# First attention layer of a two-layer cross-attention kernel: softmax sums from ones columns beside the values, and the keys' low half taken by VectorE from PSUM

## The chip, the cores and the metric

The kernel runs on one NeuronCore of a Trainium2 chip. The metric is device time in microseconds (us) of one execution of the whole program; lower is better. The core has TensorE (PE, and PEld for its weight loads), VectorE (DVE), ScalarE (ACT), GpSimd (POOL) and SyncE (SP), which here issues the DMAs. Each engine runs its own instruction list in order and waits on semaphores.

## What is computed

The input x has 8 batches of 256x512, the context has the same shape. The change touches the first layer only: attention with 16 heads of depth 16 over 512 positions, whose outputs are a weighted mean and a weighted standard deviation of the values.

```python
q = einsum('oc,bct->bot', Wq, x) + bq ; k, v likewise from kv
attn = softmax(einsum('bhqd,bhdk->bhqk', q * scale, k))       # 8 batches, 16 heads, 512 x 512
mean = einsum('bhqk,bhkd->bhqd', attn, v)
ex2  = einsum('bhqk,bhkd->bhqd', attn, v * v)
std  = sqrt(relu(ex2 - mean * mean))
out  = masked_instance_norm(x) * std + mean
```

A second layer (self attention, cross attention, MLP, each over 8 batches) follows. It isn't changed.

## The kernel before

Layer 0 works in 32 groups (`GROUPS`): 8 batches of 4 groups, each of `HG` = 4 heads. One window `w` has 8 steps `s`. In step N = 8w + s, TensorE makes the scores of group w for one block of 128 queries and two heads (L321, `scores`), in two halves (high and low parts of fp32 kept as fp32r), and, `LAG` = 13 steps later, the same scores the other way round (L333, `turned`: keys on partitions, step M = N - LAG). VectorE takes the row maxima of the first (L429, `maxima`, one reduction of 128x1024 a step); these go through `spread_maxima` (L435) and the item "turn" into the query operand of the second, so that the exponential (L559, `exponentials`, ScalarE, 128x1024 a step) needs no further subtraction. `weighted` (L345) multiplies the exponentials with `v`, which holds 16 columns of values and 16 of squared values for each head: in every second step four matmuls with 32 output columns each, one per head, in the four column groups of the array.

The PSUM banks: 0 to 3 for scores (two sets), 4 and 5 for `turned` (one set), 6 (`VB`) for `weighted`, 7 (`MB`) for all else. What goes through bank 7 is an ordered list of items (L110, `items_at`): "z" at step 0, "turn" at 1, "k" at 2, "q" at 4, "v" at 6. Each item waits for `s_free`, that is, until the item before it was read out. "k" and "q" project the next group's keys and queries, "v" projects values (two times in four windows).

The softmax sums go another way. GpSimd adds the exponentials of two steps (L657, `pairs`: 4 a window), TensorE sums these over partitions with a matrix of ones (item "z": 8 matmuls), ScalarE copies the result (`take_sums`, L601), and SP writes one row for each head to DRAM.

The next group's keys: ScalarE reads the "k" item into `raw_k` with the bias (`take_k`), VectorE rounds it to `k1` (`high_k`, L406, step 3), GpSimd subtracts (`low`, L647), and VectorE makes `k2` from the rest (`low_k`, L412, step 6). The queries go through `take_q`, `high_q` (L417, step 5) and `both_q` (L423, step 6). At the first step of a window TensorE waits for `k1`, `k2`, `q1` and `q2` of the group.

Once a batch: SP loads the next batch's context, x and mask (L229, `load`, in the window w % 4 == 2); VectorE turns the mask into `far` (L395, `masks`) and sums x and its squares; the sums go SP (`z`) - VectorE (`shares`, L483) - SP (`shares0`, then `rz`, a broadcast back); GpSimd multiplies (`finish_shares`, L666, w % 4 == 3), ScalarE squares the mean (`mean_squared`, step 3), GpSimd subtracts (`finish_variance`, L675); one window later ScalarE takes roots (`roots`, L611, step 3 of w % 4 == 0), which needs another activation table, and GpSimd ends with `finish_x`. SP's `regroup` (L234) moves `v_out` (two buffers) to `mean_in` and `second`; for the first group of a batch it waits until `finish_variance` of the batch before has run:

```python
if G == 0 and b:
    eng.wait_ge(s_fin, FINISH * (b - 1) + 3)
```

Of the kernel before, what the change touches and what calls it, by code (L numbers as in the profile page):

```python
# [7 lines left out]
F32 = mybir.dt.float32  # L8
F32R = mybir.dt.float32r
U8 = mybir.dt.uint8  # L10
ALU = mybir.AluOpType
# [89 lines left out]
def layer0(nc, d, g):  # L101

    GROUPS = NB * NG
    LAG = 13
    RING, SUMS, PROBS = 4, 6, 6
# [4 lines left out]
    def items_at(w, s):  # L110

        if s == 0 and 0 <= w - 3 < GROUPS:
            return [("z", w - 3)]
        if s == 1 and 0 <= w - 1 < GROUPS:
            return [("turn", w - 1)]
        if s in (2, 4) and w + 1 < GROUPS:
            return [("k" if s == 2 else "q", w + 1)]
        if s == 6 and w % 4 == 3 and w + 1 < GROUPS:
            return [("v", (w + 1) // 2)]
        if s == 6 and w % 4 == 1 and w < GROUPS:  # L120
            return [("v", w // 4 * 2 + 1)]
        if s == 6 and w == 0:
            return [("v", 0)]
        return []
# [4 lines left out]
    with ExitStack() as ctx:  # L129
# [9 lines left out]
        ones = sb("ones", [P, QD])  # L139
# [14 lines left out]
        v = sb("v", [P, DC, NH, 2 * HD0])  # L154
        prob = sb("prob", [P, PROBS, 2, D])
        pair = sb("pair", [P, SUMS, 2, D])
        v_out = sb("v_out", [P, 2, D])
        z_out = sb("z_out", [P, D])
# [28 lines left out]
        s_pair = sem("pair")  # L187
# [4 lines left out]
        s_low = sem("low")  # L192
# [6 lines left out]
        s_zd = sem("zd")  # L199
# [4 lines left out]
        s_re = [sem(f"re{k}") for k in range(2)]  # L204
# [16 lines left out]

        def rows_of(n):

            return slice(QD * n, QD * (n + 1))

        with nc.Block() as block:
            @block.sync
            def _(eng):
# [5 lines left out]
                def regroup(n):  # L234

                    b, G = n // NG, n % NG
                    eng.wait_ge(s_vout, n + 1)
                    if G == 0 and b:
                        eng.wait_ge(s_fin, FINISH * (b - 1) + 3)
                    for k in range(HG):  # L240
                        head = HG * (G % 2) + k
                        for j, dst in enumerate((mean_in, second)):
                            src = v_out[QD * k + HD0 * j:QD * k + HD0 * (j + 1), n % 2, :]
                            eng.dma_start(dst[HD0 * head:HD0 * (head + 1), G // 2, :], src).then_inc(s_re[n % 2], DMA)

# [8 lines left out]
                for w in range(GROUPS + 4):  # L254
                    n = w - 3
                    b, G = n // NG, n % NG
                    if 0 <= n < GROUPS:
                        taken(eng, "z", n)
                        for k in range(HG):
                            eng.dma_start(d["sums0"][b % 2, HG * G + k:HG * G + k + 1, :], z_out[QD * k:QD * k + 1, :])\  # L260
                               .then_inc(s_zd, DMA)
                        if G == NG - 1:
                            eng.wait_ge(s_zd, (n + 1) * HG * DMA)
                            eng.dma_start(z[:], d["sums0"][b % 2].rearrange("h (a e) -> (h a) e", a=P // NH))\
                               .then_inc(s_z, DMA)
# [4 lines left out]
                    if 0 <= n < GROUPS and G == NG - 1:  # L270
                        eng.wait_ge(s_rz, b + 1)
                        eng.dma_start(d["shares0"][b % 2].rearrange("h (a e) -> (h a) e", a=P // NH), z[:])\
                           .then_inc(s_rd, DMA)
                        if b:
                            eng.wait_ge(s_fin, FINISH * (b - 1) + 2)
                        eng.wait_ge(s_rd, (b + 1) * DMA)
                        for c in range(SB):
                            eng.dma_start(rz[:, c, :], d["shares0"][b % 2, NH // 2 * c:NH // 2 * (c + 1), None, :]
                                          .broadcast_to([NH // 2, HD0, D])).then_inc(s_rw, DMA)
                    if 0 <= n < GROUPS and G == 0:  # L280
                        regroup(n)
                    if 0 <= n + 1 < GROUPS and (n + 1) % NG:
                        regroup(n + 1)
# [3 lines left out]
            def _(eng):  # L287
                def item(name, n):
# [24 lines left out]
                    else:  # L313
                        eng.wait_ge(s_pair, 4 * n + 4)
                        for u in range(2):
                            for k in range(HG):
                                mm = eng.matmul(ps[rows_of(k), MB, :], ones[:], pair[:, (4 * n + 2 * u + k // 2) % SUMS, k % 2, :],  # L317
                                                start=(u == 0), stop=(u == 1))
                    mm.then_inc(s_item, 1)

                def scores(N, half):  # L321

                    n, j, p = N // 8, N % 8 // 2, N % 2
                    for i in range(2):
# [3 lines left out]
                        mm = eng.matmul(ps[:, SC + 2 * p + i, :], lhsT[r, slot, P * j:P * (j + 1)], rhs[r, n % RING, :],  # L328
# [4 lines left out]
                def turned(M, half):  # L333

                    n, c, p = M // 8, M % 8 // 2, M % 2
# [9 lines left out]
                def weighted(M):  # L345

                    n, c = M // 8, M % 8 // 2
                    b, G = n // NG, n % NG
                    eng.wait_ge(s_exp, M + 2)
                    if c == 0:  # L350
                        eng.wait_ge(s_sq, 2 * b + G // 2 + 1)
                        if n:
                            eng.wait_ge(s_vout, n)
                    for k in range(HG):
# [1239 lines left out]
```

## Time and profile before

| | |
|---|---|
| median of 3 runs | 2137.65 us (2135.59 to 2139.13) |
| the profiled execution | 2135.27 us, span 2133.4 us |
| PE / PEld busy | 1855.3 / 1192.9 us (87% / 56%) |
| DVE / ACT / POOL busy | 1422.0 / 999.7 / 708.5 us (67% / 47% / 33%) |
| mean granted TensorE clock | 0.918 of full speed |
| layer 0 | from the start to about 882 us |

Busy shares are means over four stages with different limits, so the stretch of layer 0 has to be read by itself, by its windows. The time of a window is read from one start of TensorE's `scores` after the wait at step 0 to the next.

### The profile page before, as it was taken

To read this page: it belongs to the slowest core of one execution; us is meant where nothing else is said; L and a number is where in the kernel's file an instruction comes from. 1 tells how busy PE (TensorE), PEld (TensorE's weight loads), DVE (VectorE), ACT (ScalarE), POOL (GpSimd) and SP (SyncE) were. 2 spreads that over 40 slices of the span, in tenths; PEclk is the share of its full clock that TensorE was granted. 3 is DMA by queue.
4 is the path that set the end of the run, shared out by engine and by line. 5 is a ranking of instruction groups with operands and counts; after the bars stand their busy time and mean duration, and the time that the engine had idled before them with its cause. 6 is when DMAs were issued, how large, how long until landed. Compare 5 with 4: busy or idle time off the path is not lost. (4 is left out here: it accounts for less than half of the span.)

```text
span 2133.4 us, 36040 instructions
## 1 busy us (share of the span) xinstructions
PE 1855.3 (87%) x12384; PEld 1192.9 (56%) x12384; DVE 1422.0 (67%) x2731; ACT 999.7 (47%) x2224; POOL 708.5 (33%) x557
## 2 busy tenths in 40 slices
PE   6788878787878787399999996999999969999999
PEld 2323222232222232277777774777777739999998
DVE  4877888879797974177777773777777765232232
ACT  1445555545454545165666653655556545121111
POOL 1545565656565656332222221322222203000000
PEclk8888898988888888699999998999999979999999
DMA  3101010110101000432222222322222204000000
GB/s 109 32 11 44 11 42 23 31 33 21 33 24 40 16 17 21 161 91 61 59 59 59 59 60 73 102 75 69 69 74 74 59 28 146 11 10 10 10 10 20
DMA packets 72907, 104.36 MB, mean 49 GB/s; under 512 B 21220, under 2 KB 37096, under 8 KB 72168
## 3 DMA queue, kind: packets, MB, share of 16 engines
q1 hardware_dynamic: 64616, 86.27, 13.9%
q0 software_dynamic: 8192, 16.79, 3.0%
q8 instruction: 59, 0.97, 0.2%
q14 instruction: 40, 0.33, 0.0%
HBM read 39.56 MB, written 4.72 MB: 21 GB/s over the span
## 5 line engine op out<-in xcount | busy, mean ns | idle before, releaser
L663 POOL TENSOR_TENSOR pair<-prob 128x1024 f32<-128x1024 f32 x128 | 316.5, 2477 | 318.3 <-ACT prob L565 318.3
L432 DVE TENSOR_REDUCE nmax<-ps 128x2 f32<-128x1024 f32 x256 | 310.2, 1217 | 133.7 <-PE ps L328 131.1
L565 ACT ACTIVATE prob<-ps 128x1024 f32<-128x1024 f32 x256 | 262.2, 1024 | 216.8 <-PE ps L340 208.0
L328 PE MATMUL ps<-k,q 32*128 32x512 f32 x1024 | 214.4, 499 | 107.0 <-DVE k L414 91.6
L328 PEld LDWEIGHTS ps<-k,q 32*128 32x128 f32 x1024 | 92.4, 209 | 291.6 <-issue 215.5
L1404 ACT ACTIVATE mlp_h<-ps,b 128x256 f32<-128x256 f32 x128 | 53.7, 472 | 266.8 <-PE ps L1339 266.8
L1443 DVE CAST mlp_h_hi<-mlp_h 128x512 fp32r<-128x512 f32 x64 | 30.2, 471 | 218.8 <-ACT mlp_h L1404 218.8
L340 PE MATMUL ps<-q,k 32*128 32x512 f32 x512 | 143.5, 556 | 34.4 <-ACT prob L565 34.0
L1153 ACT ACTIVATE cross_prob<-cross_t,cross_nmax 128x256 f32<-128x256 f32 x256 | 127.6, 502 | 66.8 <-DVE cross_nmax L1052 65.0
L1153 ACT ACTIVATE self_prob<-self_t,self_nmax 128x256 f32<-128x256 f32 x256 | 127.6, 502 | 55.0 <-DVE self_nmax L1052 53.4
L1339 PE MATMUL ps<-mlp_x_hi,mlp_w_hi 128*128 128x256 f32 x512 | 145.9, 285 | 6.5 <-DVE mlp_w_lo L1428 6.5
L355 PE MATMUL ps<-prob,v 128*32 128x512 f32 x1024 | 149.8, 660 | 1.1 <-ACT prob L565 1.1
L1339 PE MATMUL ps<-mlp_x_lo,mlp_w_hi 128*128 128x256 f32 x512 | 146.0, 285 | 0.0
L1339 PE MATMUL ps<-mlp_x_hi,mlp_w_lo 128*128 128x256 f32 x512 | 146.0, 285 | 0.0
L1238 POOL TENSOR_TENSOR cross_low<-cross_low,cross_high 128x512 fp32r<-128x512 f32 x32 | 41.3, 1292 | 314.4 <-DVE cross_high L1064 286.5
L317 PE MATMUL ps<-pair,ones 128*32 128x512 f32 x512 | 106.6, 980 | 24.6 <-DVE v L451 22.7
L949 PE MATMUL ps<-self_xT,w_self 128*128 128x256 f32 x512 | 125.3, 389 | 2.9 <-ACT self_xT L1175 1.1
L1052 DVE CUSTOM_DVE_ANT_0 self_t<-self_t,self_off 128x256 f32<-128x256 f32 x256 | 112.4, 476 | 18.4 <-DVE self_t L1046 0.6
L1238 POOL TENSOR_TENSOR self_low<-self_low,self_high 128x512 fp32r<-128x512 f32 x32 | 40.6, 1268 | 253.1 <-DVE self_high L1064 225.2
L1052 DVE CUSTOM_DVE_ANT_0 cross_t<-cross_t,cross_off 128x256 f32<-128x256 f32 x256 | 109.2, 463 | 18.4 <-DVE cross_t L1046 0.2
L340 PE MATMUL ps<-q2m,k 32*128 32x512 f32 x512 | 113.1, 436 | 0.0
L949 PEld LDWEIGHTS ps<-self_xT,w_self 128*128 128x128 f32 x512 | 93.7, 192 | 20.2 <-ACT self_low L1167 5.1
(182 smaller groups left out, 4367.5 us busy)
## 6 DMA issues: line engine op xcount, KB each, us to landing
self_k_stack<-self_high SPq DMA_DIRECT2D x128, 64.0 KB, 2.1
cross_k_stack<-cross_high SPq DMA_DIRECT2D x128, 64.0 KB, 2.1
mlp_w_in<-in_w SPq DMA_DIRECT2D x32, 256.0 KB, 3.0
c_in<-in_ctx SPq DMA_DIRECT2D x8, 512.0 KB, 3.7
X<-in_x SPq DMA_DIRECT2D x8, 512.0 KB, 4.5
mean_in<-v_out SPq DMA_DIRECT2D x128, 32.0 KB, 2.0
second<-v_out SPq DMA_DIRECT2D x128, 32.0 KB, 2.0
rz<-shares SPq DMA_DIRECT2D x16, 256.0 KB
```

The lines of the kernel that those rows point to most:

```text
L317: mm = eng.matmul(ps[rows_of(k), MB, :], ones[:], pair[:, (4 * n + 2 * u + k // 2) % SUMS, k % 2, :], start=(u == 0), stop=(u == 1))
L328: mm = eng.matmul(ps[:, SC + 2 * p + i, :], lhsT[r, slot, P * j:P * (j + 1)], rhs[r, n % RING, :], start=(half == 0), stop=(half == 1))
L340: mm = eng.matmul(ps[:, ST + i, :], lhsT[r, n % RING, P * c:P * (c + 1)], rhs[r, slot, :], start=(half == 0), stop=(half == 1))
L355: mm = eng.matmul(ps[rows_of(k), VB, :], v[:, c, HG * G + k, :], prob[:, (M + k // 2) % PROBS, k % 2, :], start=(c == 0), stop=(c == DC - 1))
L432: eng.tensor_reduce(nmax[:, n % 2, j, 2 * p:2 * p + 2], ps[:, SC + 2 * p:SC + 2 * p + 2, :], AX, ALU.max, negate=True).then_inc(s_max, 1)
L565: eng.activation(prob[:, M % PROBS, :, :], ps[:, ST:ST + 2, :], ACT.Exp).then_inc(s_exp, 1)
L663: eng.tensor_tensor(pair[:, at % SUMS, :, :], prob[:, M % PROBS, :, :], prob[:, (M + 2) % PROBS, :, :], ALU.add).then_inc(s_pair, 1)
L949: mm = eng.matmul(bank[:, S * T:S * (T + 1)], wt[:, c, P * (2 * n + T):P * (2 * n + T + 1)], src[:, c, :], start=(c == 0), stop=(c == DC - 1))
L1052: ins = eng.tensor_tensor_reduce(t[:, i, k, :], t[:, i, k, :], off[:, j, :], 1.0, NEVER, ALU.add, ALU.min, nmax[:, m % 4, k:k + 1])
L1153: ins = eng.activation(prob[:, m % 2, i, :], t[:, p, i, :], ACT.Exp, scale=-1.0, bias=nmax[:, m % 4, i:i + 1], accum_out=z[:, T % 2, j, 2 ...
L1238: eng.tensor_tensor(low[:, k, :, :], low[:, k, :, :].bitcast(F32), high[:, k, :, :].bitcast(F32), ALU.subtract).then_inc(s_lo.sem, 1)
L1339: mm = eng.matmul(ps[:, HB + n % 2, S * i:S * (i + 1)], w[:, c, col], x[:, c, :], start=(k == 0), stop=(k == len(terms) - 1))
```

## The change

- `v` gets 64 columns for each head: values, squares, and 32 columns of ones that are set once. `weighted` has 64 output columns a matmul, so that a bank of 128 partitions holds two heads; a group of four heads is done in two passes of four steps each. The sums come out of the same matmuls. `pairs`, the item "z", `take_sums`, `pair` and `z_out` are gone.
- Steps are ordered so that the four blocks of one pair of heads follow each other; `LAG` is 12. `v_out` has three buffers (`OUTS`), read out twice a window (steps 1 and 5); `regroup` issues 6 DMAs a pass, sums among them.
- The keys' high and low parts are both made by VectorE straight from PSUM (`high_k`, now two instructions, step 2), `low_k` moves to step 3, `high_q` to 4, `both_q` to 5. `take_k` and GpSimd's `low` are gone.
- Items: "k" at step 1, "turn" at 2, "q" at 3, "v" at 5.
- SP's order: in w % 4 == 1 the whole chain from the sums to `rz` comes before the next window's `load`, where before `load` stood between `z` and its wait for `shares`.

```diff
-    LAG = 13
-    RING, SUMS, PROBS = 4, 6, 6
+    LAG = 12
+    RING, PROBS, OUTS = 4, 6, 3
...
-        if s == 0 and 0 <= w - 3 < GROUPS:
-            return [("z", w - 3)]
-        if s == 1 and 0 <= w - 1 < GROUPS:
+        if s in (1, 3) and w + 1 < GROUPS:
+            return [("k" if s == 1 else "q", w + 1)]
+        if s == 2 and 0 <= w - 1 < GROUPS:
             return [("turn", w - 1)]
...
-        v = sb("v", [P, DC, NH, 2 * HD0])
+        v = sb("v", [P, DC, NH, 4 * HD0])
...
                 def regroup(n):
 
-                    b, G = n // NG, n % NG
+                    b, G, p = n // (2 * NG), n // 2 % NG, n % 2
                     eng.wait_ge(s_vout, n + 1)
-                    if G == 0 and b:
+                    if G == 0 and p == 0 and b:
                         eng.wait_ge(s_fin, FINISH * (b - 1) + 3)
...
+                for w in range(GROUPS + 3):
                     if w % NG == 2 and w + 2 < GROUPS:
                         made(eng, "k", w + 1)
                         eng.wait_ge(s_mask, w // NG + 1)
                         load(w // NG + 1)
...
+                    if 0 <= w - 2 < GROUPS:
+                        n = w - 2
+                        b, G = n // NG, n % NG
+                        regroup(2 * n)
+                        regroup(2 * n + 1)
+                        if G == NG - 1:
+                            for k in range(OUTS):
+                                eng.wait_ge(s_re[k], regrouped(2 * n + 1, k))
+                            eng.dma_start(z[:], d["sums0"][b % 2].rearrange("h (a e) -> (h a) e", a=P // NH))\
+                               .then_inc(s_z, DMA)
+                            eng.wait_ge(s_rz, b + 1)
...
                 def weighted(M):
 
-                    n, c = M // 8, M % 8 // 2
+                    n, c, p = M // 8, M % 4, M % 8 // 4
                     b, G = n // NG, n % NG
-                    eng.wait_ge(s_exp, M + 2)
                     if c == 0:
                         eng.wait_ge(s_sq, 2 * b + G // 2 + 1)
-                        if n:
-                            eng.wait_ge(s_vout, n)
-                    for k in range(HG):
-                        mm = eng.matmul(ps[rows_of(k), VB, :], v[:, c, HG * G + k, :], prob[:, (M + k // 2) % PROBS, k % 2, :],
-                                        start=(c == 0), stop=(c == DC - 1))
+                        if 2 * n + p:
+                            eng.wait_ge(s_vout, 2 * n + p)
+                    for m in range(M, M + 2):
+                        eng.wait_ge(s_exp, m + 1)
+                        for k in range(2):
+                            mm = eng.matmul(ps[2 * QD * k:2 * QD * (k + 1), VB, :], v[:, m % 4, HG * G + 2 * p + k, :],
+                                            prob[:, m % PROBS, k, :], start=(m % 4 == 0), stop=(m % 4 == 3))
                     mm.then_inc(s_pv, 1)
...
                 def high_k(n):
-                    taken(eng, "k", n)
+                    made(eng, "k", n)
                     if n >= RING:
                         eng.wait_ge(s_st, 8 * (n - RING) + 8)
-                    eng.tensor_copy(k1[:, n % RING, :], raw_k[:]).then_inc(s_k1, 1)
+                    eng.tensor_scalar(k1[:, n % RING, :], ps[:, MB, :], b0[:, 1, n % NG:n % NG + 1], None, ALU.add)\
+                       .then_inc(s_k1, 1)
+                    eng.wait_ge(s_k1, n + 1)
+                    eng.scalar_tensor_tensor(out=raw_k[:], in0=ps[:, MB, :], scalar=b0[:, 1, n % NG:n % NG + 1],
+                                             in1=k1[:, n % RING, :].bitcast(F32), op0=ALU.add, op1=ALU.subtract)\
+                       .then_inc(s_free, 1)
...
                 def take_values(n):
-                    eng.wait_ge(s_pv, 4 * n + 4)
-                    if n >= 2:
-                        eng.wait_ge(s_re[n % 2], (n // 2) * 2 * HG * DMA)
-                    eng.activation(v_out[:, n % 2, :], ps[:, VB, :], ACT.Copy).then_inc(s_vout, 1)
+                    eng.wait_ge(s_pv, 2 * n + 2)
+                    if n >= OUTS:
+                        eng.wait_ge(s_re[n % OUTS], n // OUTS * 6 * DMA)
+                    eng.activation(v_out[:, n % OUTS, :], ps[:, VB, :], ACT.Copy).then_inc(s_vout, 1)
```

## Rows read from the trace of the kernel before

**Rows 1.** Stretches of layer 0: bounds, length, busy time by engine, PEclk, DMA share, GB/s.
```profile
100.05:204.18 104.13, 81.79 (x533) 29.95 (x534) 80.11 (x77) 48.66 (x57) 56.01 (x26) 0.84 0.09 25
204.18:716.27 512.09, 407.37 (x2660) 150.29 (x2661) 432.13 (x441) 261.93 (x305) 299.92 (x135) 0.85 0.10 28
716.27:793.04 76.77, 61.63 (x391) 21.98 (x392) 63.14 (x68) 39.47 (x46) 41.08 (x19) 0.83 0.07 18
793.04:844.66 51.62, 40.03 (x254) 12.91 (x254) 28.05 (x40) 30.03 (x33) 35.07 (x15) 0.84 0.09 21
```

**Rows 2.** Groups of instructions by line: busy, mean ns; idle before, with releasers.
```profile
L663 POOL TENSOR_TENSOR pair<-prob 128x1024 f32<-128x1024 f32 x128 | 316.5, 2477 | 318.3 <-ACT prob L565 318.3
L328 PE MATMUL ps<-k,q 32*128 32x512 f32 x1024 | 214.4, 499 | 107.0 <-DVE k L414 91.6 <-DVE nmax L432 15.4
L451 DVE TENSOR_TENSOR v<-ps,bv 128x512 f32<-128x512 f32 x16 | 10.9, 683 | 0.0
```

**Rows 3.** Timeline at a window's end (start, length, engine): DVE beside GpSimd.
```profile
406.15 2.82 DVE L414 SCALAR_TENSOR_TENSOR k<-raw_k,row,far 128x512 fp32r<-128x512 f32 x1
...
409.07 0.80 PE L328 MATMUL ps<-k,q 32*128 32x512 f32 x2 [4.01 <-DVE k L414]
```

**Rows 4.** Timeline of one window, w = 14: its first steps.
```profile
357.34 0.74 DVE L414 SCALAR_TENSOR_TENSOR k<-raw_k,row,far 128x512 fp32r<-128x512 f32 x1
...
366.53 0.50 PE L309 MATMUL ps<-q,ident_r 128*128 128x512 f32 x1
...
367.36 0.50 PE L328 MATMUL ps<-k,q 32*128 32x512 f32 x2
...
370.03 0.50 PE L328 MATMUL ps<-k,q 32*128 32x512 f32 x2
```

**Rows 5.** The same window, a step with `weighted` and the next with "q".
```profile
370.70 1.06 PE L355 MATMUL ps<-prob,v 128*32 128x512 f32 x8
370.81 1.22 DVE L432 TENSOR_REDUCE nmax<-ps 128x2 f32<-128x1024 f32 x1 [1.45 <-PE ps L328]
370.85 1.02 ACT L565 ACTIVATE prob<-ps 128x1024 f32<-128x1024 f32 x1
...
371.92 0.50 PE L340 MATMUL ps<-q,k 32*128 32x512 f32 x2
...
372.58 1.98 PE L300 MATMUL ps<-X,w 128*128 128x512 f32 x4
```

**Rows 6.** Timeline of the drain, where "z" met the full clock.
```profile
811.39 1.92 PE L317 MATMUL ps<-pair,ones 128*32 128x512 f32 x16
...
813.25 0.50 PE L340 MATMUL ps<-q,k 32*128 32x512 f32 x2
```

**Rows 7.** SP's queue and what stands beside it, windows w = 14 and 15.
```profile
370.13 0.41 SPq L230 DMA_DIRECT2D c_in<-in_ctx  x1
...
378.91 0.34 SPq L272 DMA_DIRECT2D shares<-z  x1
...
380.42 1.29 SPq L278 DMA_DIRECT2D rz<-shares  x2
...
405.75 0.58 SPq L244 DMA_DIRECT2D mean_in<-v_out  x1
```

**Rows 8.** DMA issues: count, KB each, median us from issue to landing.
```profile
m_in<-in_mask SPq DMA_DIRECT2D x8, 64.0 KB, 4.4
...
mean_in<-v_out SPq DMA_DIRECT2D x128, 32.0 KB, 2.0
```

**Rows 9.** Timeline at layer 0's end: from the sums to their shares' use.
```profile
857.70 1.31 SPq L278 DMA_DIRECT2D rz<-shares  x2
862.93 2.34 POOL L671 TENSOR_TENSOR mean_a<-mean_in,rz 128x1024 f32<-128x1024 f32 x1 [15.38 <-DMA rz<-shares]
```

**Rows 10.** Timeline of w = 16, step 3: the roots in ScalarE's queue.
```profile
421.38 1.28 ACT L614 ACT_TABLE_LOAD   x1
...
425.14 1.02 ACT L565 ACTIVATE prob<-ps 128x1024 f32<-128x1024 f32 x1
```

More of the change, by code:

```diff
@@ L153, in layer0 @@
         wide = sb("wide", [P, DC, P], F32R)
-        v = sb("v", [P, DC, NH, 2 * HD0])
+        v = sb("v", [P, DC, NH, 4 * HD0])
         prob = sb("prob", [P, PROBS, 2, D])
-        pair = sb("pair", [P, SUMS, 2, D])
-        v_out = sb("v_out", [P, 2, D])
-        z_out = sb("z_out", [P, D])
+        v_out = sb("v_out", [P, OUTS, D])
         z = sb("z", [P, NH * D // P])
@@ L186, in layer0 @@
         s_exp = sem("exp")
-        s_pair = sem("pair")
         s_pv = sem("pv")
@@ L203, in layer0 @@
         s_rw = sem("rw")
-        s_re = [sem(f"re{k}") for k in range(2)]
+        s_re = [sem(f"re{k}") for k in range(OUTS)]
         s_mask = sem("mask")
@@ L220, in made, with regrouped @@
             eng.wait_ge(s_item, number[(name, n)] + 1)
+        def regrouped(n, k):
+            return (n - k + OUTS) // OUTS * 6 * DMA
         def rows_of(n):
@@ L269, in _ @@
                         load(w // NG + 1)
[L270 to L283, printed above, removed]
+                    if 0 <= w - 2 < GROUPS:
[9 more added lines that the diff above has]
+                            eng.wait_ge(s_rz, b + 1)
+                            eng.dma_start(d["shares0"][b % 2].rearrange("h (a e) -> (h a) e", a=P // NH), z[:])\
+                               .then_inc(s_rd, DMA)
+                            if b:
+                                eng.wait_ge(s_fin, FINISH * (b - 1) + 2)
+                            eng.wait_ge(s_rd, (b + 1) * DMA)
+                            for c in range(SB):
+                                eng.dma_start(rz[:, c, :], d["shares0"][b % 2, NH // 2 * c:NH // 2 * (c + 1), None, :]
+                                              .broadcast_to([NH // 2, HD0, D])).then_inc(s_rw, DMA)
                 eng.wait_ge(s_big, 4 * DMA)
@@ L312, in item @@
                                             stop=(j == DC - 1))
[L313 to L318, printed above, removed]
                     mm.then_inc(s_item, 1)
                 def scores(N, half):
-                    n, j, p = N // 8, N % 8 // 2, N % 2
+                    n, j, p = N // 8, N % 4, N % 8 // 4
                     for i in range(2):
@@ L617, in _ @@
                 eng.wait_ge(s_b0, 1)
-                take_k(0)
                 take_q(0)
@@ L655, in squares @@
                     eng.tensor_tensor(v[:, :, half, HD0:2 * HD0], vv, vv, ALU.mult).then_inc(s_sq, 1)
-                def pairs(n, u, p):
-                    at, M = 4 * n + 2 * u + p, 8 * n + 4 * u + p
-                    eng.wait_ge(s_exp, M + 3)
-                    if at >= SUMS:
-                        made(eng, "z", (at - SUMS) // 4)
-                    eng.tensor_tensor(pair[:, at % SUMS, :, :], prob[:, M % PROBS, :, :], prob[:, (M + 2) % PROBS, :, :],
-                                      ALU.add).then_inc(s_pair, 1)
                 def finish_shares(b, k):
                     if k == 0:
-                        for n in range(2):
-                            eng.wait_ge(s_re[n], (b + 1) * NG // 2 * 2 * HG * DMA)
+                        for k in range(OUTS):
+                            eng.wait_ge(s_re[k], regrouped(2 * NG * b + 2 * NG - 1, k))
                         eng.wait_ge(s_rw, (b + 1) * SB * DMA)
```

114 lines of the change are left out of this document (37 added, 77 removed).

## The prediction

> **What bounds the kernel now.** Only layer 0 changes, so I read it by itself, first by stretches. Between TensorE's first `scores` of w = 8 and of w = 28 lie five batches in 512.09 us, 102.4 each or 25.6 a window [rows 1]. VectorE is busy 432 of these 512 us, TensorE 407, at a mean granted clock of 0.85: part of the time runs at the lower level (1.2 instead of 2.4 GHz). Neither engine is full, so the order of work decides. The groups by line say where TensorE stands: 91.6 us idle in front of `scores`, waiting for the next group's `k2` [rows 2]. The timeline of a window's end shows why: `low_k` comes last before the window starts, takes 2.82 us beside a GpSimd addition [rows 3], and 0.74 us where none runs [rows 4]. After 4.01 us of waiting TensorE's matmuls take 0.80 us instead of 0.50 [rows 3, 4]: it has also lost its clock. So a window is eight steps plus a stall of about 4 us and its echo.
>
> **The steps, priced at full clock.** The four pieces of `scores` and `turned` fill 0.67 us before `weighted` begins (370.03 to 370.70) [rows 4, 5]. The exponential starts at 370.85, takes 1.02, and the next `turned` starts at 371.92, 1.89 after the step's own start at 370.03: no step can be shorter, since banks 4 and 5 exist once and `turned` and the exponential take turns in them [rows 4, 5]. A step with "k" or "q" is 0.67 + 1.95 = 2.62 (one such step: 2.67 [rows 4]). "turn" adds 0.83 (366.53 to 367.36) [rows 4].
>
> **What is removed.** GpSimd's `pairs` (128 of 2477 ns [rows 2]) were never the last to arrive; they count by what they did to `low_k` and the other VectorE operations beside them. The item "z" (8 matmuls with four column groups at work) takes 1.86 at full clock (811.39 to 813.25) [rows 6] and goes. The wait for `k2` goes: `low_k` now follows at step 3, `both_q` at step 5, two steps ahead of need. In all, the stall and its clock echo of every window.
>
> **What is added.** (1) `weighted`: four matmuls with 32 columns take one turn of the array's four column groups, about 1.0; now two matmuls share it, so four of them make two turns. I price them as what "z" shows, two turns in 1.86, less a little, 1.84 [rows 6]: 0.85 more than before, 128 times. The bounds: 1.0 if width were free [rows 5], and 3.9 if each matmul of 64 columns ran alone like those of "k" (two in 1.95 [rows 4, 5]). I take 1.84, since time per turn doesn't depend on the columns used in any of these rows. With `scores` the step is 2.51.
> (2) VectorE's `high_k` reads bank 7 twice, after `maxima` of step 2. A PSUM operand of that size costs 0.68 [rows 2]; two cost 1.36. "turn" is next in bank 7, in the same step 2. Its wait ends at 0.78 (scores done, 370.81 less 370.03) + 1.22 + 1.36 + 0.04 = 3.4 after the step's start [rows 4, 5], where TensorE is free at 2.51: a new stall of 0.9 in every window, and the step is 3.4 + 0.83 = 4.23.
> (3) ScalarE loses `take_k` and `take_sums`, gains a second `take_values`: nothing, it stays off the path in plain windows.
>
> The Trainium skill (SBUF — State Buffer, Who interferes with whom) says that a VectorE operation with two SBUF inputs, or in a two-port mode, waits for a GpSimd one in full; the trace agrees, 2.82 against 0.74 [rows 3, 4]. By it the new subtraction, with one input in PSUM, would never wait.
>
> **A plain window:** steps 0, 4, 6: 3 x 2.51; steps 1, 3: 2 x 2.62; step 2: 4.23; steps 5, 7: 2 x 1.89. Sum 20.8, against 25.6. Two "v" items a batch add 0.75 each: 4 x 20.8 + 1.5 = 84.7 a batch, 17.7 less than now. VectorE's work fits: no step asks more than 3.4 of it.
>
> **Once a batch, four places give much of it back.**
> (a) The load. Before, SP issued it at 370.13, ahead of `shares` at 378.91 and `rz` at 380.42 [rows 7]. Now it comes behind them. Counted from step 5 of w % 4 == 2: `maxima` ends at 2.0, `both_q` and `shares` at 3.2, `rz` is issued at 3.2 + 1.5 = 4.7, `load` at 6.0, its last part at 7.0, landing 4.4 later = 11.4 [rows 7, 8]; but `rz` itself lands 5.2 after its issue [rows 9], about 9.9, and the load's bytes queue behind it. I take 12.5. TensorE wants it at step 1 of the next window, at 1.89 + 2.51 + 1.89 + 2.51 + 0.67 = 9.5. Stall 3.0, in six batches, plus 0.6 for VectorE's `masks`, which wait for the same load and stand in front of `maxima` of step 2.
> (b) `take_values` at step 5 of w % 4 == 3. With three buffers it needs the one whose `regroup` is the first of the batch, and that waits for `finish_variance`. From the start of step 4: `take_q` and then `mean_squared` end at 1.85 (about 0.7 and 1.05 in ScalarE's queue; the exponential of step 4, due at 0.82, is 1.0 late, and 0.6 of that is slack of a 2.51 step over 1.89: 0.4 lost), `finish_variance` at 4.4 (2.34 when nothing is beside it [rows 9], 2.5 taken), then six DMAs of up to 0.6 each [rows 7], the last landing 2.0 after its issue [rows 8]: 8.9. ScalarE is there at 4.8 and has the exponential of step 6 queued behind; TensorE stands at `weighted` of step 6 from 6.2 until 9.6. Stall 3.4 + 0.4, in seven batches. Before, this regroup began at 405.75 [rows 7], with a whole window left.
> (c) `roots` at step 3: table, roots, table, then the exponential 3.76 later (421.38 to 425.14) [rows 10]. It now comes behind `take_q`, so the exponential due at 0.82 starts at 0.8 + 3.76 = 4.56, 3.7 late; less 0.6 of slack TensorE loses 3.1 (it loses some of that before too, inside the 102.4).
> (d) Each of these three pauses is as long as the one after which the matmuls slowed [rows 3]. I take 1.7 for each dip of the clock, an estimate between nothing and the 2.5 that a whole step of `weighted` would lose at half clock: 5.1.
> A batch: 84.7 + 3.6 + 3.8 + 3.1 + 5.1 = 100.3, against 102.4: 2.1 less.
>
> **The sum.** Batches 2 to 6: 5 x 2.1 = 10.5. Batch 1 has no roots: 84.7 + 7.4 + 3.4 = 95.5 against 104.1: 8.6 [rows 1]. Windows 28 to 30 (no load): 62.4 + 0.8 + 3.1 + 1.7 = 68.0 against 76.8: 8.8 [rows 1]. From w = 31 to the last exponential: 51.6 now [rows 1]; about 55.4 by the same steps, for "k", "q" and their stall were already absent and `weighted` costs more: minus 3.8. Behind it the last pair additions and "z" drop out of the chain of sums, and a regroup comes in: 1.8 less. The first batch (pipeline filling, hardly a stall or a "z") at nothing. 10.5 + 8.6 + 8.8 - 3.8 + 1.8 = 26. The profiled execution took 2135.27 (span 2133.4), 2.4 below the median of 2137.65, within their spread. 2135.3 - 26 = 2109; I say 2109.
>
> **The rivals.**
> 1. The giving back doesn't happen: the load's bytes overtake, or the regroup of (b) is early enough, and the clock stays high. Then a batch is 84.7 + 3.1 = 87.8: 14.6 less, five times 73, batch 1 19.4, windows 28 to 30 10.9, the end nothing: 103 less, 2032. For it: medians of DMA latency come from busy times. Against it: both orders are fixed in the code, and the sums are several us over.
> 2. Slower, by the price of 64 columns. If two 64-column matmuls don't share the array fully, each `weighted` costs more than 1.84; at 1.84 + 26/128 = 2.04 the gain is gone, at 3.9 the kernel takes 2109 + 128 x 2.06 = 2373, at a halfway 2.9 it is 2245. Nothing in the trace shows a 64-column tile. Against it: the two ends in the trace both fill the array.
> A page weighs for it: the Trainium skill (TensorE: Matmul & The Clock Gate, Measured speedup vs the span model) gives 2.38 times for three tiles of 32 columns, not 3. Here four tiles gain more, 4 in 1.0 against 2 in 1.95 at full width, 3.9 times, so the trace doesn't bear it out. By that shortfall (0.79) `weighted` would take about 2.3, and the kernel, by the rows, 2109 + 128 x 0.46 = 2168.
> 3. Slower, by the batch stalls: if load and regroup each cost 3 us more than I say (a load that shares the queue with `rz` throughout, the wait for it also holding VectorE), thirteen times 3 are 39: 2148. It decides from 2 us more on.
> 4. It doesn't do what it says: the stall in front of a window stays at 4 us because another of the four semaphores comes last. In the 29 windows from w = 2 on that prepare a next one, 29 x 4 = 116 more than my sum: 2225. Against it: `both_q` is done at step 5.
>
> **How the numbers follow.** The forecast, a gain mostly given back, 0.5 (its own range 2085 to 2132); rival 1, whole or in good part, 0.2; rival 2 0.12 (its page's version 0.04 of that); rival 3 0.13; rival 4 0.05. About 0.2% (4 us) is what a measurement of this kernel can tell from no change. Faster: 0.2 + nine tenths of 0.5 + a bit = 0.66; within: 0.12; slower: 0.22. The range takes in rival 1 and rival 3: 2030 to 2152.
>
> **What would show it.** Right: `weighted` steps of 2.5; a 0.9 us wait in front of "turn" on VectorE's `high_k`; no wait of `scores` for `k2`; one wait a batch of "k" for the load and one of `weighted` for `v_out`; `low_k` at 0.74; GpSimd busy less than half of now; a mean clock of 0.85 to 0.95 in layer 0. Wrong: `weighted` steps of 3 or more; a layer 0 that ends before 830 us or after 890 (now about 882).

## The result, and the profile after

The changed kernel takes 2145.99 us (median of 18 runs, 2137.45 to 2155.15); the kernel before takes 2137.77 in the same rounds (18 runs, 2135.59 to 2140.21). The ratio is 1.0038, with a 95% interval of 1.0026 to 1.0050: slower by 0.4%, where 2109 and a gain of 1.3% were forecast.

The page of the changed kernel, its first part (engine, busy us, share, instructions) and the costliest groups of layer 0 (busy, mean ns | idle before, releaser):

```profile
span 2135.6 us, 34721 instructions
PE 1868.5 (87%) x11872; PEld 1214.7 (57%) x11872; DVE 1288.7 (60%) x2763; ACT 973.5 (46%) x2192; POOL 343.5 (16%) x397
...
L345 PE MATMUL ps<-prob,v 128*64 128x512 f32 x1024 | 270.7, 652 | 24.8 <-issue 20.8
L317 PE MATMUL ps<-k,q 32*128 32x512 f32 x1024 | 201.3, 469 | 8.7 <-DVE nmax L427 4.6
```

By shares, the change did what it says. GpSimd's busy time halves (708.5 to 343.5), VectorE loses 133 us, and the idle time in front of `scores` falls from 107.0 us [rows 2] to 8.7. Not even the clock speaks against it: over the program the granted clock rises from 0.918 to 0.948. Yet nothing is won, so the question is where the 98 us of removed stall went, and with it the forecast gain of 26. The groups of layer 0 by line, of the same trace, name the heirs:

```profile
L295 PE MATMUL ps<-c_in,w 128*128 128x512 f32 x128 | 77.6, 738 | 36.4 <-DMA m_in<-in_mask 36.4
L588 ACT ACTIVATE v_out<-ps 128x512 f32<-128x512 f32 x64 | 37.9, 593 | 31.3 <-DMA second<-v_out 30.1 <-PE ps L345 1.2
L304 PE MATMUL ps<-q,ident_r 128*128 128x512 f32 x32 | 16.3, 510 | 29.6 <-DVE raw_k L403 29.6
```

The "k" item waits for the load (11.1 of the 36.4 us at the very start, 25.3 in six batches), the read-out into `v_out` waits for a `regroup` (30.1 in seven batches), and "turn" waits for VectorE's second read of bank 7 (29.6 us over 32 windows, 0.9 in most of them). All three stand in the forecast. So the miss is one of sizes, and it takes an account stretch by stretch.

**The account.** I cut both traces as the forecast did, at TensorE's first `scores` of a window; layer 0 ends where VectorE starts on the next layer's first tile. "Usual" is a second execution of the changed kernel (2144.24 us, e9 below); the first profiled one is the fastest of the 18 and shows only 2.2 of the 8 us.

| stretch | forecast | fastest execution | usual execution |
|---|---|---|---|
| start to w = 4 | 0 | +8.5 | +8.5 |
| w = 4 to 8 (batch 1) | -8.6 | -5.9 | -4.2 |
| w = 8 to 28 (batches 2 to 6) | -10.5 | -1.2 | +3.4 |
| w = 28 to 31 | -8.8 | -7.2 | -8.4 |
| w = 31 to the end of layer 0 | +2.0 | +4.1 | +6.3 |
| the rest of the program | 0 | +4.0 | +3.3 |
| sum | -26 | +2.2 | +9.0 |

(The spans are 2133.4 before, 2135.6 and 2142.4 after; the rows are rounded. The bounds before are 100.05, 204.18, 716.27, 793.04 [rows 1] and 882.7; in the changed kernel they are 108.50, 206.72, 717.60, 787.13 and 880.9, in e9 108.50, 208.47, 723.99, 792.41 and 888.4.)

**A plain window is as forecast.** Timeline of the changed kernel from step 0 of w = 17 to the "q" item at step 3 (start, length, engine, line, output and inputs, idle before):

```profile
439.73 1.94 PE L345 MATMUL ps<-prob,v 128*64 128x512 f32 x8
...
441.59 0.50 PE L317 MATMUL ps<-k,q 32*128 32x512 f32 x2
...
444.17 0.50 PE L317 MATMUL ps<-k,q 32*128 32x512 f32 x2
...
446.09 0.74 DVE L400 TENSOR_SCALAR k<-ps,b 128x512 fp32r<-128x512 f32 x1
...
446.87 0.75 DVE L403 SCALAR_TENSOR_TENSOR raw_k<-ps,b,k 128x512 f32<-128x512 f32 x1
447.67 0.50 PE L304 MATMUL ps<-q,ident_r 128*128 128x512 f32 x1 [0.89 <-DVE raw_k L403]
...
449.26 1.99 PE L295 MATMUL ps<-X,w 128*128 128x512 f32 x4
...
450.41 0.74 DVE L409 SCALAR_TENSOR_TENSOR k<-raw_k,row,far 128x512 fp32r<-128x512 f32 x1
```

`weighted` occupies 439.73 to 441.59, 1.86 (forecast 1.84). The wait in front of "turn" is 0.89 (0.9). `low_k` takes 0.74, where it took 2.82 beside GpSimd [rows 3]. From one "q" item to the next, windows without a batch's event take 20.95, or 21.72 with "v" (20.8 and 21.5).

### The profile page after: what moved, and what is told of

Same layout as the page of the kernel before. It is cut to its first block and busy times, and to the rows that moved or that the text cites. A ratio compares the mean times of both kernels' runs of the same rounds, so it can differ in the third digit from the quotient of the medians.

```text
span 2135.6 us, 34721 instructions
## 1 busy us (share of the span) xinstructions
PE 1868.5 (87%) x11872; PEld 1214.7 (57%) x11872; DVE 1288.7 (60%) x2763; ACT 973.5 (46%) x2192; POOL 343.5 (16%) x397
## 5 line engine op out<-in xcount | busy, mean ns | idle before, releaser
L345 PE MATMUL ps<-prob,v 128*64 128x512 f32 x1024 | 270.7, 652 | 24.8 <-issue 20.8
L317 PE MATMUL ps<-k,q 32*128 32x512 f32 x1024 | 201.3, 469 | 8.7 <-DVE nmax L427 4.6
L329 PE MATMUL ps<-q,k 32*128 32x512 f32 x512 | 134.4, 521 | 65.7 <-ACT prob L561 65.7
L317 PEld LDWEIGHTS ps<-k,q 32*128 32x128 f32 x1024 | 86.9, 197 | 157.5 <-DVE nmax L427 99.2
L1397 DVE CAST mlp_h_hi<-mlp_h 128x512 fp32r<-128x512 f32 x64 | 30.1, 470 | 218.8 <-ACT mlp_h L1358 218.8
L345 PEld LDWEIGHTS ps<-prob,v 128*64 128x64 f32 x1024 | 66.2, 143 | 154.2 <-issue 147.7
L295 PE MATMUL ps<-c_in,w 128*128 128x512 f32 x128 | 77.6, 738 | 36.4 <-DMA m_in<-in_mask 36.4
L329 PEld LDWEIGHTS ps<-q,k 32*128 32x128 f32 x512 | 49.9, 192 | 98.9 <-ACT prob L561 92.6
L329 PE MATMUL ps<-q2m,k 32*128 32x512 f32 x512 | 105.3, 408 | 0.0
L1293 PEld LDWEIGHTS ps<-mlp_x_hi,mlp_w_hi 128*128 128x128 f32 x512 | 99.0, 193 | 9.5 <-DVE mlp_w_lo L1382 7.4
```

The source lines that it names most:

```text
L295: mm = eng.matmul(bank, (wq if name == "q" else wk)[:, c, P * G:P * (G + 1)], src, start=(c == 0), stop=(c == SB - 1))
L317: mm = eng.matmul(ps[:, SC + 2 * (N % 2) + i, :], lhsT[r, slot, P * j:P * (j + 1)], rhs[r, n % RING, :], start=(half == 0), stop=(half == 1))
L329: mm = eng.matmul(ps[:, ST + i, :], lhsT[r, n % RING, P * c:P * (c + 1)], rhs[r, slot, :], start=(half == 0), stop=(half == 1))
L345: mm = eng.matmul(ps[2 * QD * k:2 * QD * (k + 1), VB, :], v[:, m % 4, HG * G + 2 * p + k, :], prob[:, m % PROBS, k, :], start=(m % 4 == 0) ...
L1293: mm = eng.matmul(ps[:, HB + n % 2, S * i:S * (i + 1)], w[:, c, col], x[:, c, :], start=(k == 0), stop=(k == len(terms) - 1))
```

## The experiments

Single windows are cut here at the starts of the "q" items: window w runs from the "q" of w - 1 to its own. The stall of the load then falls into w % 4 == 3, that of `v_out` (from step 5 of that window) into w % 4 == 0, and that of the roots into w % 4 == 1.

**e1: the load no longer behind `rz`.** The load is issued first, the shares' way out and back (`shares0`, `rz`) moves behind it, out of w % 4 == 1:

```diff
+                def shared_out(b):
+                    eng.wait_ge(s_rz, b + 1)
+                    eng.dma_start(d["shares0"][b % 2].rearrange("h (a e) -> (h a) e", a=P // NH), z[:])\
+                       .then_inc(s_rd, DMA)
...
+                    if w % NG == 2 and 0 <= w - 3 < GROUPS:
+                        shared_out((w - 3) // NG)
```

> The changed kernel with one order on SP put back: the next batch's load is issued before SP waits for the shares, as in the kernel before. Theory 1 (in plain windows the change gains 4 to 5 us each, and it gives that back at three places a batch, each with its echo in the clock): the wait of the k item for the load (25 us over six batches in the trace of after, 3.8 to 4.7 each) is gone, and with the clock echo six windows of 26.0 to 28.1 us between two q items become about 21.3; 6 x 5.5 = 33 us less than the changed kernel's median of 2146, so about 2113. Rival (another wait takes its place: TensorE's doubled weighted sum is the real limit): within 10 us of 2146. The spread of the runs, 18 us in the changed kernel, should shrink if it comes from DMA latencies on the path.

Measured: 2138.07 us (10 runs, 2135.3 to 2150.19), ratio to before 1.0007 [0.9992, 1.0023], 8 us less than the changed kernel and not 33. The rival's number (within 10 us of 2146) came true, but the next limit is not `weighted`, as it had it. The spread did not shrink much either: 15 us over 10 runs. The wait of "k" is gone (11.1 us are left, at the start), and another took its place. Timeline of e1 around step 1 and 2 of w = 19:

```profile
483.74 2.36 POOL L640 TENSOR_TENSOR mean_a<-mean_in,rz 128x1024 f32<-128x1024 f32 x1 [23.80 <-DMA rz<-shares]
...
484.51 1.87 DVE L392 CAST mask<-m_in 128x512 f32<-128x512 uint8 x1
...
486.06 2.53 POOL L642 TENSOR_TENSOR second<-second,rz 128x1024 f32<-128x1024 f32 x1
...
486.42 2.45 DVE L396 TENSOR_SCALAR far<-mask,row 128x512 f32<-128x512 f32 x1
...
488.90 1.22 DVE L431 TENSOR_REDUCE nmax<-ps 128x2 f32<-128x1024 f32 x1
...
491.63 0.80 PE L308 MATMUL ps<-q,ident_r 128*128 128x512 f32 x1 [3.85 <-DVE raw_k L407]
```

`masks` now run at step 1, where GpSimd multiplies in `finish_shares`. They take 1.87 and 2.45 us, `maxima` of step 2 stands behind them, `high_k` behind that, and "turn" waits 3.85 instead of 0.89. The load's stall had been hiding this one: `masks` waited for the same load and then met only the second of GpSimd's two multiplications (the conversion took 1.98 there, `far` 0.55). The wait for `raw_k` sums to 47.5 us here, 18 more than in the changed kernel.

**e2: a fourth `v_out` buffer.** One character, `OUTS = 3` to `OUTS = 4`, so the read-out of a batch's third last pass no longer needs the buffer whose `regroup` waits for `finish_variance`.

```diff
-    RING, PROBS, OUTS = 4, 6, 3
+    RING, PROBS, OUTS = 4, 6, 4
```

> The changed kernel with four v_out buffers instead of three, nothing else. Theory 1: ScalarE's take_values no longer waits for the regroup behind finish_variance (30 us over seven batches, 4.3 each in the trace of after), and the seven windows of 27.1 us become about 21.7: 7 x 5.4 = 38 us less, about 2108. Rival (SP is behind anyway, so the wait comes one buffer later): less than 10 us gained.

Measured: 2109.2 us (4 runs, 2108.18 to 2112.96), ratio 0.9869 [0.9852, 0.9885], 37 less than the changed kernel. The groups of layer 0 in e2 show the one wait gone and the other unchanged or longer:

```profile
L295 PE MATMUL ps<-c_in,w 128*128 128x512 f32 x128 | 78.7, 746 | 40.0 <-DMA m_in<-in_mask 40.0
...
L588 ACT ACTIVATE v_out<-ps 128x512 f32<-128x512 f32 x64 | 37.9, 592 | 1.2 <-PE ps L345 1.2
```

The windows w % 4 == 0 fall from 27.1 to 21.96, so this stall and its clock echo cost 5.2 each, seven times: 36. The forecast had 3.8 + 1.7 = 5.5, and the expectation of 38 us less was met.

**e3: both.**

> Both edits in one: load issued first and four v_out buffers. Theory 1: the gains add, since they lie in different windows: about 71 us less than the changed kernel, about 2075, with 29 windows near 21 us but those with the roots (26.7). Rival: the gains overlap (each dip of the clock is shared by two stalls) and the sum is under 50, over 2096.

Measured: 2091.88 us (4 runs, 2085.96 to 2095.25), ratio 0.9774 [0.9755, 0.9792], between the two expectations. In e3 "turn" waits 3.99 at the same place as in e1: `masks` beside `finish_shares` hold on to 28 us (what e6 wins over e3) of the 45 that lie between e2 and e6.

**e6: `masks` one step earlier.** On top of e3, `masks` move from step 1 to step 7 of the window before, where GpSimd is idle (with the load in time, the mask is there).

```diff
+                        if w % NG == 2 and s == 7 and b + 1 < NB:
+                            masks(b + 1)
...
-                            if s == 1 and b + 1 < NB:
-                                masks(b + 1)
```

> e3_both with the mask work of the next batch (two VectorE instructions) moved from step 1 of the window w % 4 == 3 to step 7 of the window before. In e1 and e3 the wait for the load is gone, but the six windows w % 4 == 3 still take 24.4 to 25.4 us instead of 21: the mask copy (1.9 to 2.0 us there, 0.43 alone) and the far operation (2.45, alone 0.55) meet finish_shares on GpSimd and hold maxima and high_k of step 2, and turn waits 3.9 us. Theory 1, extended (the late load hid this port conflict): these windows fall to about 21.1, and with them the next window's 23.0 by 1 to 2 (its clock dip): 6 x 4 to 6 = 24 to 36 us less than e3's 2092, so 2056 to 2068. Rival (the stall moves on to another VectorE operation of these windows, since GpSimd's five large operations must run somewhere): less than 10 us gained.

Measured: 2063.96 us (4 runs, 2063.67 to 2064.31), ratio 0.9650 [0.9634, 0.9667]. The windows w % 4 == 3 are plain now (20.95). Groups of layer 0 in e6, and behind them the conversion in the changed kernel:

```profile
L308 PE MATMUL ps<-q,ident_r 128*128 128x512 f32 x32 | 16.3, 510 | 29.2 <-DVE raw_k L407 29.2
...
L396 DVE TENSOR_SCALAR far<-mask,row 128x512 f32<-128x512 f32 x8 | 4.4, 546 | 0.3
L392 DVE CAST mask<-m_in 128x512 f32<-128x512 uint8 x8 | 3.4, 422 | 1.4 <-DMA m_in<-in_mask 1.4
```

```profile
L388 DVE CAST mask<-m_in 128x512 f32<-128x512 uint8 x8 | 14.3, 1786 | 18.5 <-DMA m_in<-in_mask 18.5
```

The conversion of the mask takes 422 ns on average, against 1786 in the changed kernel, and 1.87 us in e1's timeline: same instruction, same tile, only the neighbour on GpSimd is gone. The Trainium skill (SBUF — State Buffer, Who interferes with whom) counts conversions and operations with a scalar among those that can take the pair of ports which VectorE shares with GpSimd; the engine that asks second then waits until the other's instruction is over. The traces agree, with 1786 against 422 ns for the one and 2.45 against 0.55 us for the other; in e1 the conversion ends at 486.38 and `far` at 488.87, each 0.3 us behind the end of a GpSimd multiplication (486.10 and 488.59). It is the same rule that I had quoted for `low_k`, not applied to `masks`.

**e7: no square roots in layer 0.** e6 with the two roots of a batch turned into copies, so that the activation table stays. This kernel leaves the square roots of layer 0 out; all other work is there.

```diff
-                    eng.activation(std_a[:], std_a[:], ACT.Sqrt)
-                    eng.activation(x_var[:, b, :], x_var[:, b, :], ACT.Sqrt).then_inc(s_root, 1)
+                    eng.activation(std_a[:], std_a[:], ACT.Copy)
+                    eng.activation(x_var[:, b, :], x_var[:, b, :], ACT.Copy).then_inc(s_root, 1)
```

> e6_mask_early with the two square roots of layer 0 left out (the activations copy instead), which takes away the two changes of the activation table at step 3 of w % 4 == 0 and nothing else; its output is not the reference's. It prices the third place. Theory 1: the six windows with roots (25.7 us in e3) fall to about 21.1 by the two table loads on the path and the clock's echo; 6 x 4.5 = 27 us less than e6. Rival (take_q, mean and root work itself hold ScalarE, not the tables): under 10 us less.

Measured: 2029.42 us (4 runs, 2027.33 to 2033.8), ratio 0.9492 [0.9476, 0.9508]: 34.5 less than e6, 4.9 for each of seven batches. I had expected 27 on record; the forecast's own terms (c) and (d), 3.1 + 1.7 = 4.8, for seven batches, were the better guess. Stretches of e6 and then e7 (length, busy time of PE, PEld, DVE, ACT and POOL, PEclk, DMA share, GB/s):

```profile
200.00:700.00 500.00, 434.40 (x2556) 171.92 (x2552) 359.21 (x507) 270.20 (x314) 73.86 (x37) 0.96 0.11 30
```

```profile
200.00:700.00 500.00, 444.83 (x2722) 178.18 (x2720) 392.52 (x533) 271.33 (x322) 79.88 (x40) 1.00 0.12 32
```

With the last pause gone the granted clock is 1.00 throughout: every dip that e6 still had in the steady part of this layer came with the roots.

**e8: items reordered.** e6 with "turn" at step 1, "k" at 3, "q" at 5 and "v" at 7, and VectorE's steps moved along, so that `high_k` is not between "k" and "turn" within two steps.

```diff
-        if s in (1, 3) and w + 1 < GROUPS:
-            return [("k" if s == 1 else "q", w + 1)]
-        if s == 2 and 0 <= w - 1 < GROUPS:
+        if s in (3, 5) and w + 1 < GROUPS:
+            return [("k" if s == 3 else "q", w + 1)]
+        if s == 1 and 0 <= w - 1 < GROUPS:
...
-                            if s == 2:
+                            if s == 4:
                                 high_k(w + 1)
```

> e6_mask_early with the items in another order: turn at step 1, k at 3, q at 5, v at 7 (before 2, 1, 3, 5), with the VectorE and ScalarE work that belongs to them moved along (values one step later, high_q and both_q together at step 6). It takes turn out of the same step as high_k's two reads of bank 7. Theory 1: step 1 hides the 0.83 us of turn under the exponential's 1.89, the 0.9 us wait for high_k goes, so a plain window falls from 20.95 to about 19.2, that is 1.8 us less in some 29 windows, 52 us less than e6. Rival: both_q now ends about as the next window starts, and a wait of scores for q1 takes back half or more of it, under 26 us.

Measured: 2015.39 us (4 runs, 2013.79 to 2016.65), ratio 0.9423 [0.9407, 0.9439]. The best version, 5.8% faster than before and 6.1% faster than the changed kernel. The wait in front of "turn" is 1.4 us in all 32 windows together:

```profile
L308 PE MATMUL ps<-q,ident_r 128*128 128x512 f32 x32 | 16.1, 502 | 1.4 <-DVE v L452 1.4
```

A plain window takes 19.38 where e6 has 20.95 (19.2 was expected). Of the 49 us, 28 are that wait (29.2 to 1.4); the other 21 I have not divided. "turn"'s own 0.8 us now stands in a step held by the exponential, as expected.

It also says something on the first batch. TensorE's first `scores` of w = 4 start at 108.50 in the changed kernel, 109.88 in e6, 103.86 in e8 and 100.05 before. So the order of the items alone is worth 6.0 us there, and e8 has won back 4.6 of the 8.5 us that the changed kernel had lost.

**e4: the keys alone.** The kernel before, with `high_k` in two reads of PSUM and `low_k` a step later, `take_k` and GpSimd's `low` gone; `pairs` and "z" stay.

```diff
-                    taken(eng, "k", n)
+                    made(eng, "k", n)
...
-                    eng.tensor_copy(k1[:, n % RING, :], raw_k[:]).then_inc(s_k1, 1)
+                    eng.tensor_scalar(k1[:, n % RING, :], ps[:, MB, :], b0[:, 1, n % NG:n % NG + 1], None, ALU.add)\
+                       .then_inc(s_k1, 1)
...
+                            if s == 4:
+                                low_k(w + 1)
...
-                                low_k(w + 1)
```

> The kernel before with the second part of the change alone: VectorE makes the keys' high and low parts straight from PSUM at step 3, low_k moves from step 6 to step 4, and GpSimd's subtraction and ScalarE's take_k are gone; the softmax sums still go through GpSimd's pair sums and item z. Theory 1: the stall in front of a window (91.6 us over 30 windows, plus the clock echo) came from the order of low_k, not from the sums as such. both_q is now last, done about as the window starts even at 1.7 us beside GpSimd; the window falls from 25.6 to about 22.8, held by VectorE (21.6 busy in a window of before): about 80 us less than before, 2058, far below the changed kernel. Rival (GpSimd's additions beside VectorE are the cause, so the stall stays, now on both_q): less than 25 us gained on before, over 2113.

Measured: 2131.63 us (10 runs, 2120.92 to 2135.79), ratio 0.9963 [0.9947, 0.9980]: 7 less than the 2138.70 of before in the same rounds, where 80 were expected and the rival said less than 25. Timeline of e4 in one window:

```profile
399.93 3.49 PE L299 MATMUL ps<-X,w 128*128 128x512 f32 x4 [4.16 <-DVE raw_k L412]
...
409.92 2.28 DVE L446 CAST wide<-nmax 128x16 fp32r<-128x16 f32 x1
...
412.23 2.27 DVE L448 TENSOR_TENSOR wide<-nmax,wide 128x16 fp32r<-128x16 f32 x1
...
415.15 3.64 PE L316 MATMUL ps<-pair,ones 128*32 128x512 f32 x16 [4.64 <-DVE v L457]
```

The stall for `k2` is gone (91.6 us [rows 2], now 4.1) and comes back in front of "q" and "z", 51.4 and 42.7 us over the layer. With `pairs` on GpSimd, small VectorE operations that take 0.18 and 0.19 without them (439.21 and 439.42 in the changed kernel) take 2.28 and 2.27; the wait of "z" above follows right behind these two. In front of "q", VectorE was late with its work on the mask and x and with `maxima`, so there the order counts as well. So my account of the removed stall was half a reason: the keys' way alone gives little. Taking `pairs` out alone, with the keys' way as before, was not run, so what it is worth by itself is not shown.

**e9 and e10: the changed kernel twice more.** No edit, one profiled execution each.

> The changed kernel itself, once more under the profiler: its first profiled execution was the fastest of eighteen, 8.5 us under their median, so it can't show where a usual execution spends those 8.5 us. If the spread comes from the two batch waits on DMAs, an execution of 2143 us or more shows longer waits in front of the copy to v_out (30.1 us over seven) or of the k item (25.3 over six), window by window, and the same plain windows of 21.7. If it comes from the clock, the waits are the same, and the stages after layer 0 show a lower granted clock than 0.97 in 882 to 1311.

> The changed kernel a third time under the profiler, for the same question: by the waits, its time follows the sum of the two DMA waits of layer 0; by the clock, it follows the granted clock of the stretches after layer 0.

Measured: 2144.24 and 2140.73 us. In e9 layer 0 ends at 888.4 instead of 880.9, and the rest of the program is 0.7 us shorter: all of the difference of 6.8 lies in layer 0. Plain windows are 21.72 with "v" in all three executions, the wait for `v_out` is 29.9 (30.1), and the windows w % 4 == 3 take 28.2 on average where the fastest execution took 26.7. The load's wait is the one that differs; groups of layer 0 in e9:

```profile
L295 PE MATMUL ps<-c_in,w 128*128 128x512 f32 x128 | 79.2, 750 | 42.4 <-DMA m_in<-in_mask 42.4
...
L588 ACT ACTIVATE v_out<-ps 128x512 f32<-128x512 f32 x64 | 37.9, 593 | 31.1 <-DMA second<-v_out 29.9 <-PE ps L345 1.2
```

The same place (w = 19) in the timeline of the changed kernel's fastest execution, then in e9:

```profile
480.08 1.31 SPq L277 DMA_DIRECT2D rz<-shares  x2
...
482.44 0.47 SPq L229 DMA_DIRECT2D m_in<-in_mask  x1
...
485.77 2.34 POOL L636 TENSOR_TENSOR mean_a<-mean_in,rz 128x1024 f32<-128x1024 f32 x1 [24.15 <-DMA rz<-shares]
...
488.82 3.42 PE L295 MATMUL ps<-c_in,w 128*128 128x512 f32 x4 [3.83 <-DMA m_in<-in_mask]
```

```profile
483.02 1.31 SPq L277 DMA_DIRECT2D rz<-shares  x2
...
485.38 0.54 SPq L229 DMA_DIRECT2D m_in<-in_mask  x1
...
489.76 2.34 POOL L636 TENSOR_TENSOR mean_a<-mean_in,rz 128x1024 f32<-128x1024 f32 x1 [25.20 <-DMA rz<-shares]
...
492.95 2.05 PE L295 MATMUL ps<-c_in,w 128*128 128x512 f32 x2 [5.02 <-DMA m_in<-in_mask]
```

From the issue of `rz` to its use are 5.7 us in the one and 6.7 in the other, from the load's last issue to "k" 6.4 and 7.6. The issues themselves are equally spaced. The landing itself, from the issue of `m_in` in batches 2 to 7, took 5.7 to 7.1 us in the fastest execution and 7.1 to 7.6 in e9; in e1, where the load is issued first, 4.3 to 5.0. So `rz` ahead of it in the queue is what makes the load late, and in e9 it is 6.0 of layer 0's 7.5 us. e10 lies between: 38.4 us of load wait, layer 0's end at 884.2; its clock in 700 to 880 is 0.81 against 0.85, which is part of it.

Where the scatter of this kernel comes from (18 us over 18 runs, where before has 5) is not shown by this. e6 waits for no load and no `regroup` and has 0.6 us over 4 runs, but e3 waits for neither and has 9 over 4, e2 keeps the load's wait and has 5 over 4, and e4, without either wait, has 15 over 10. One difference between e3 and e6 is that e3's `masks` run beside `finish_shares`, which starts when `rz` has landed; no run tests that.

## Why the prediction was wrong, by its own steps

**What held.** The price of `weighted` (1.86 for 1.84), the stall of "turn" (0.89 for 0.9), the plain window (20.95 for 20.8), the end of the waiting for `k2`, the places of all three batch stalls, and the windows 28 to 30 (-8.4 for -8.8). GpSimd is busy less than half of before, as said; layer 0 ends at 880.9 to 888.4, inside the bounds that I had set as "not wrong" and outside of the gain. Rivals 1, 2 and 4 are out: the giving back happens, the 64 columns cost 1.86, and `scores` waits 8.7 us in all. The Trainium skill (TensorE: Matmul & The Clock Gate, Measured speedup vs the span model) gives 2.38 times for three column tiles, from which the forecast had worked out 2.3 for rival 2; the trace does not agree, with 1.86. (Rival 1's 10.9 for the windows 28 to 30 is 10.5 by its own terms, 76.8 - 66.3, which changes nothing.)

**What failed, in order of size, for a usual execution (35 us in all, 26 of forecast gain and 9 of loss).**

1. *The batch's sum of 100.3, term (a).* Batches 2 to 6 gave +3.4 instead of -10.5, and batch 1 -4.2 instead of -8.6. From "q" to "q" (w = 7 to 27) a usual batch takes 103.3 (fastest execution 102.2), and before takes 102.1. Against the forecast the plain windows have 85.3 for 84.7; the load's stall with its echo 28.2 - 20.95 = 7.3 (fastest 5.7) for 3.6 + 1.7 = 5.3; the regroup's 27.3 - 21.72 = 5.6 (5.4) for 5.5; the roots' 26.1 - 20.95 = 5.1 (5.8) for 4.8. So 2.0 of the 3.0 is the load; in batch 1 the load's stall is 29.3 - 20.95 = 8.4, 3.1 over. The step that failed in it is the landing time. I had the issues right: the last part at 7.0 after step 5's start, and it is issued at 482.44, 7.0 after 475.42. I then set the landing at 12.5; it lands at 13.3, "k" starts at 13.4 after that point, and over a microsecond later in a usual execution. The term for the bytes of `rz` ahead of it was too small: 6.25 from issue to landing here and 7.4 in e9, where 12.5 allowed 5.5. And the time of `rz` came from a row of the drain, 5.2 [rows 9], where nothing follows in the queue; here it is 5.7 and 6.7.
2. *The first batch "at nothing".* +8.5. This is the step with the least reason. By window starts, w = 0 is 2.6 us longer than before, w = 1 8.5 longer (25.0 for 16.4), w = 2 3.7 shorter and w = 3 1.0 longer. In w = 1 the pipeline fills at the low clock: each of "k" and "q" takes 3.8 us, and the two reads of `high_k` come between "k" and whatever is next in bank 7. Timeline of the changed kernel, w = 1, and the same "k" and "q" in the kernel before:

```profile
43.57 3.78 PE L295 MATMUL ps<-c_in,w 128*128 128x512 f32 x4
...
51.27 0.80 PE L304 MATMUL ps<-q,ident_r 128*128 128x512 f32 x1 [2.77 <-DVE raw_k L403]
...
53.89 3.78 PE L295 MATMUL ps<-X,w 128*128 128x512 f32 x4
```

```profile
42.05 3.56 PE L300 MATMUL ps<-c_in,w 128*128 128x512 f32 x4
...
46.38 1.98 PE L300 MATMUL ps<-X,w 128*128 128x512 f32 x4
```

   The wait for "turn" is 2.77 here, not 0.9, and "q" takes 3.78 as "k" did, where before it takes 1.98, at the full clock. Against before, where "turn" waits 0.30 in this window, these two are 2.5 and 1.8 us, 4.3 of w = 1's 8.5. That is read from the trace; no run tests it alone, and e8, which moves the items, wins back 4.6 in all. A term that is zero "because hardly anything happens there" has to be looked up like the others.
3. *The end of the layer.* +6.3 (fastest +4.1) for +2.0. From the first `scores` of w = 31 to the last exponential's end it takes 60.8 us (58.6), where I had 55.4 "by the same steps"; behind it the chain is 2.9 (2.8) shorter than before, for 1.8. The granted clock of that stretch is 0.80 (0.88), and 0.84 before; I haven't followed it event by event.
4. *The rest of the program.* +3.3 to +4.0, where I had nothing. In each of the three executions of the changed kernel the stages after layer 0 take 1254.0 to 1254.7 us, before 1250.7; e6 has 1253.8 and e8 1254.9. The text of these stages is the same. The table by windows puts it into two places, the first 40 us of the second layer (granted clock 0.86 for 0.89) and the change of stage near 1300 (0.71 for 0.79). Why the dips fall longer there, in e4 too (1253.6) and least in e7 (1252.6), stays open.
5. *The profiled execution.* The 2109 is the profiled execution of before less the 26; from its median of 2137.65 the same sum gives 2111.7. And the first profile of the changed kernel is the fastest of 18 and lies 8.5 below the median. That is what e9 is for: of a kernel that scatters by 18 us, one profile shows one draw.

**Rival 3 was the closest.** It said 3 us more in each of load and regroup and gave 2148. It was one of the two, by 2 us in a usual batch and 3 in the first, and not 3 in both; the rest of its 39 us came from items 2 to 4. So its time was right in good part by luck, with half of the reasons. What it also missed is e1: taking the load's stall away alone gives little, since the next wait, `masks` beside GpSimd, is 3 us late at the same place. The forecast wrote 0.6 for `masks`, and the port they share with `finish_shares` not at all, though [rows 3] shows it for `low_k`.

**Where the gain is.** The three steps from the changed kernel to e6 cost one buffer, one move on SP and one on VectorE, and are worth 82 us; e8's order is worth another 49, of which the wait of "turn" is 28. What the change contributes to this is not isolated: that these gains need `pairs` gone is argued from e4, which has the keys' part without it and gains 7.

## What to carry to other kernels

When a change removes a stall of every window, list what is next to arrive once a batch, and test the transfers among these first: here each that had been a whole window ahead and was now within one cost 5 to 8 us a batch with its clock echo. Take a transfer's landing time from a place where the same transfers stand ahead of it in its queue, not from a median or from a drain. And when a wait is removed, look at which operations it had kept apart: here a late load had kept `far` out of GpSimd's way.

## What the hardware showed that I had not expected

- Four matmuls of 64 columns (two column groups of the array each) take 1.86 us, four of 32 columns about 1.0 [rows 5], two of full width 1.95: the time goes by the columns occupied, within 5%.
- A conversion of one 128x512 tile from bytes takes 0.42 us alone (e6) and 1.87 us beside a GpSimd multiplication (e1); one of 128x16 takes 0.18 and 2.28. A VectorE operation reading PSUM and one SBUF tile (`high_k`'s second, 0.75) was never stretched, also not in e4, where GpSimd was busy for the whole length of 29 of 32 of them (0.751 on average).
- The square roots, with their two table loads of 1.28 us [rows 10], cost 4.9 us a batch: a pause in the exponentials, and TensorE's clock, which is 1.00 from 200 to 700 us without them and 0.96 with them.
- `rz` (two transfers of 256 KB) ahead of the load in the queue moves the load's landing from 4.3 to 5.0 us after its last issue (e1, load first; 4.4 before [rows 8]) to 5.7 to 7.1, and to 7.1 to 7.6 in another execution of the same program (e9).
